# Softmax denominators of a graph-attention and expert kernel: in the last block of queries VectorE adds the weights of the second key head and of every fourth chunk of the first

## The reference

```python
h = _rmsnorm(x, ln1_w)
q = (h @ wq.T)...; k = (h @ wk.T)...; v = (h @ wv.T)...   # 4 query heads, 2 key heads, 32 channels each
scores = jnp.einsum('bhtd,bhsd->bhts', q, k) / jnp.sqrt(jnp.float32(HD))
scores = jnp.where(causal[None, None], scores, jnp.float32(-1e+30))
att = jax.nn.softmax(scores, axis=-1)
y = jnp.einsum('bhts,bhsd->bhtd', att, v)
x = x + y @ wo.T
# then a router picks 2 of 8 experts for each token, and the experts' outputs are added
```

## Time and profile before

| | us |
|---|---|
| median of 3 runs | 4142.93 |
| lowest, highest | 4135.64, 4162.34 |
| the profiled execution, its own time | 4167.11 |
| its span, first to last instruction | 4165.5 |
| TensorE busy (share of the span) | 3452.7 (83%) |
| VectorE busy | 2752.5 (66%) |
| ScalarE busy | 1306.4 (31%) |
| POOL busy | 1638.8 (39%) |
| mean granted TensorE clock, of full | 0.911 |

### The profile page before, as it was taken

How to read it: one execution, slowest core, us unless ns; L and a number is a source line. 1 busy time by engine, 2 the same in 40 slices (tenths; PEclk the granted TensorE clock), 3 DMA queues, 4 the chain that set the end, 5 groups by cost and what they waited for, 6 DMA issues and landing times. The chain is left out here.

```text
span 4165.5 us, 48116 instructions
## 1 busy us (share of the span) xinstructions
PE 3452.7 (83%) x16381; PEld 1324.3 (32%) x16381; DVE 2752.5 (66%) x3882; ACT 1306.4 (31%) x1635; POOL 1638.8 (39%) x1016
## 2 busy tenths in 40 slices
PE   1456899999999859987999899999899999839960
PEld 1233444444444312222222222222222222105540
DVE  8778887614344457777778878777777775326752
ACT  0000000000000014433444455454445455625640
POOL 1000000000000014544766486565478566844551
PEclk8567899999999969999999999999999999969985
DMA  9888998787888436500100000000000000012225
GB/s 372 347 346 346 345 344 319 288 292 284 296 296 291 169 123 236 181 10 5 33 13 6 12 21 8 10 1 10 1 23 9 6 1 6 12 54 65 75 65 181
DMA packets 165282, 572.71 MB, mean 137 GB/s; under 512 B 20193, under 2 KB 55786, under 8 KB 114550
## 3 DMA queue, kind: packets, MB, share of 16 engines
q1 hardware_dynamic: 91304, 457.35, 29.7%
q10 hardware_dynamic: 60432, 88.88, 6.0%
q0 software_dynamic: 13360, 24.03, 1.8%
HBM read 478.22 MB, written 90.57 MB: 137 GB/s over the span
## 5 line engine op out<-in xcount | busy, mean ns | idle before, releaser
L958 DVE TENSOR_REDUCE unit_max<-ps_max 128x1 f32<-128x512 f32 (+3 forms) x2176 | 1356.6, 662 | 424.2 <-PE ps_max L1215 306.6
L786 POOL TENSOR_TENSOR chunk_sum<-chunk_sum,probs 128x1024 f32<-128x1024 f32 (+1 forms) x528 | 1196.1, 2265 | 577.4 <-ACT probs L918 563.2
L918 ACT ACTIVATE probs<-ps_scores 128x1024 f32<-128x1024 f32 (+1 forms) x1088 | 1020.9, 984 | 1057.2 <-PE ps_scores L1234 858.4
L1215 PE MATMUL ps_max<-keep_k_stack,q_stack 96*128 96x512 f16 (+3 forms) x2176 | 762.1, 383 | 154.4 <-DVE unit_max L958 114.1
L1234 PE MATMUL ps_scores<-q_stack,keep_k_stack 97*128 97x512 f16 (+3 forms) x2176 | 616.1, 378 | 36.4 <-ACT probs L918 32.6
L1245 PE MATMUL ps_out<-probs,keep_v 128*32 128x512 f32 (+3 forms) x4352 | 567.2, 594 | 0.6 <-ACT probs L918 0.6
L314 DVE TENSOR_TENSOR partial_degree<-partial_degree,ring 128x2048 f32<-128x2048 f32 x240 | 550.0, 2292 | 7.1
L1215 PEld LDWEIGHTS ps_max<-keep_k_stack,q_stack 96*128 96x128 f16 x2176 | 182.2, 97 | 974.8 <-DVE unit_max L958 822.2
L497 PE MATMUL ps_gather<-ring,keep_attended 128*128 128x512 f32 x960 | 449.2, 630 | 22.1 <-DVE keep_attended L338 22.1
L512 PE MATMUL ps_gather_low<-ring,keep_attended 128*128 128x512 f32 x800 | 362.2, 609 | 1.4 <-DVE keep_attended L338 1.4
L277 POOL DMA_DIRECT2D scratch_lower<-lower x15 | 9.3, 618 | 815.7 <-ACT lower L416 815.7
(11 more groups left out here) (232 smaller groups left out, 2709.7 us busy)
## 6 DMA issues: line engine op xcount, KB each, us to landing
ring<-in_adj SPq DMA_DIRECT2D x392, 1024.0 KB, 6.7
scratch_slots<-empty_rows ACTq DMA_DIRECT2D x16, 2080.0 KB, 7.4
scratch_parts<-empty_part ACTq DMA_DIRECT2D x8, 2048.0 KB, 7.6
moe_parts<-scratch_parts SPq DMA_DIRECT2D x64, 256.0 KB, 3.5
moe_x_rows<-scratch_slots SPq DMA_DIRECT2D x39, 260.0 KB
x_in<-in_x SPq DMA_DIRECT2D x16, 256.0 KB, 6.0
x_in<-in_x ACTq DMA_DIRECT2D x16, 256.0 KB, 9.9
cos<-in_cos ACTq DMA_DIRECT2D x16, 256.0 KB, 8.0
```

The lines of the kernel that those rows point to most:

```text
L786: nc.gpsimd.tensor_tensor(chunk_sum[:, :, lo:], chunk_sum[:, :, lo:], weights, ALU.add).then_inc(chunk_added, 1)
L918: nc.scalar.activation(probs[:, j, kv, :, lo:], ps_scores[kv][:, :, lo:], ACT.Exp, scale=SCALE).then_inc(exp_done, 1)
L958: nc.vector.tensor_reduce(unit_max[:, i, at:at + 1], bank[:, 0:width], AX_X, ALU.max).then_inc(bank_free, 1)
L1215: last = nc.tensor.matmul(out[:, 0:width], q_stack[0:SHIFT_ROW, T % QBUF, h, s * P:(s + 1) * P], k_stack[0:SHIFT_ROW, h // NREP, G * BT:G ...
```

## The change

In the units 121 to 135 (`late_units`, all of the last block but the diagonal) three things differ.

- TensorE no longer calls `add_weights`; `weigh` itself counts `chunk_used` up by one for each chunk.
- VectorE gets `add_late`, after the last of the four steps of each chunk: it adds the chunk's `kv` = 1 weights into the new SBUF tile `late_sums[:, 1]`, and at the fourth chunk also the `kv` = 0 weights into `late_sums[:, 0]`. The first add of each half is a copy. That is 75 operations on 128 x 1024 float32 (73 adds and 2 copies), five for each of 15 units; each add waits for the one before it by `late_added`.
- POOL skips its add at the fourth chunk of each late unit (it only counts the semaphore), so it makes 45 adds there where it made 60.

ScalarE waits for `late_added` before it overwrites a part of `probs` that VectorE reads. At the end of the block TensorE waits for all 75 and adds `late_sums` to the total with four more matmuls.

```diff
--- before.py
+++ after.py
@@ -612,6 +612,8 @@
         paces.append(1 if LAST - 1 in Rs else 2)
         scattered_at.append(routed_at[-1] + 4 * paces[-1])
 
+    late_units = range(first_unit(LAST) + 1, first_unit(NB))
+
     def preparing(unit):
 
         for R in range(LAST):
@@ -649,6 +651,7 @@
         q_stack = sb("q_stack", [STACK, QBUF, NH, BT], F16)
         probs = sb("probs", [P, SUB, NKV, NREP, BT])
         chunk_sum = sb("chunk_sum", [P, NREP, BT])
+        late_sums = sb("late_sums", [P, NKV, NREP, BT])
         zeros = sb("zeros", [SHIFT_ROW, P], F16)
         even_and_odd = sb("even_and_odd", [P, P])
         unit_max = sb("unit_max", [P, TILES, NB + 1])
@@ -702,6 +705,7 @@
         exp_done = sem("exp_done")
         chunk_used = sem("chunk_used")
         chunk_added = sem("chunk_added")
+        late_added = sem("late_added")
         numerator_copied = sem("numerator_copied")
         sums_copied = sem("sums_copied")
         combined = sem("combined")
@@ -841,7 +845,11 @@
             for T in range(NB):
                 for n, G in enumerate(units_of(T)):
                     for j in range(SUB):
-                        add_chunk(T, first_unit(T) + n, j, n == 0)
+                        if first_unit(T) + n in late_units and j == SUB - 1:
+                            pool.wait_ge(chunk_added, (first_unit(T) + n) * SUB + j)
+                            pool.sem_inc(chunk_added, 1)
+                        else:
+                            add_chunk(T, first_unit(T) + n, j, n == 0)
                         route(first_unit(T) + n, j)
             divide(LAST)
             keep_residual(LAST)
@@ -915,6 +923,8 @@
                         act.wait_ge(chunk_used, unit * SUB + (j - SUB + 1))
                         if kv == 0:
                             act.wait_ge(chunk_added, unit * SUB + (j - SUB + 1))
+                        if unit - 1 in late_units and (kv or j == SUB - 1):
+                            act.wait_ge(late_added, (SUB + 1) * (unit - 1 - late_units[0]) + j + 1 + (kv == 0))
                     nc.scalar.activation(probs[:, j, kv, :, lo:], ps_scores[kv][:, :, lo:], ACT.Exp,
                                          scale=SCALE).then_inc(exp_done, 1)
 
@@ -973,6 +983,20 @@
                 if T >= KEPT:
                     dve.wait_ge(block_divided, T - KEPT + 1)
                 nc.vector.tensor_copy(denominators[:, T % KEPT], ps_sum[:]).then_inc(sums_kept, 1)
+
+            def add_late(unit, j):
+
+                first = unit == late_units[0]
+                for kv in ((1, 0) if j == SUB - 1 else (1,)):
+                    dve.wait_ge(exp_done, unit * EXPS + PER_CHUNK * j + kv + 1)
+                    before = (SUB + 1) * (unit - late_units[0]) + j + (kv == 0)
+                    out, weights = late_sums[:, kv], probs[:, j, kv]
+                    if first and (j == 0 or kv == 0):
+                        add = nc.vector.tensor_copy(out, weights)
+                    else:
+                        dve.wait_ge(late_added, before)
+                        add = nc.vector.tensor_tensor(out, out, weights, ALU.add)
+                    add.then_inc(late_added, 1)
 
             def invert(R, s):
                 here = denominators[:, R % KEPT, s * P:(s + 1) * P]
@@ -1171,6 +1195,8 @@
                         if T and v == 0 and i == COMBINE_GAP:
                             keep_denominators(T - 1)
                         route(first_unit(T) + v, i)
+                        if first_unit(T) + v in late_units and i % SUB == SUB - 1:
+                            add_late(first_unit(T) + v, i // SUB)
                 if T == 0:
                     round_shift(1)
             b = len(batches) - 1
@@ -1272,6 +1298,13 @@
                 for r in range(NREP):
                     last = nc.tensor.matmul(ps_sum[r * HD:(r + 1) * HD, :], keep["ones_heads"][:], chunk_sum[:, r, :],
                                             start=False, stop=True, skip_group_check=True)
+                if T == LAST:
+                    pe.wait_ge(late_added, (SUB + 1) * len(late_units))
+                    for kv in range(NKV):
+                        for r in range(NREP):
+                            at = kv * NREP + r
+                            last = nc.tensor.matmul(ps_sum[at * HD:(at + 1) * HD, :], keep["ones_heads"][:],
+                                                    late_sums[:, kv, r, :], start=False, stop=True, skip_group_check=True)
                 last.then_inc(combined, 1)
 
             def project(R):
@@ -1339,7 +1372,8 @@
                     for kv in range(NKV):
                         scores(T, unit, G, 0, kv, True)
                 for j in range(SUB):
-                    paired = not diagonal and j % 2
+                    late = unit in late_units
+                    paired = not diagonal and j % 2 and not late
                     for kv in range(NKV):
                         if j + 1 < SUB:
                             scores(T, unit, G, j + 1, kv, diagonal)
@@ -1350,13 +1384,15 @@
                     pe.wait_ge(exp_done, unit * EXPS + PER_CHUNK * (j + 1))
                     if diagonal and j == 0 and T:
                         pe.wait_ge(numerator_copied, T)
-                    weigh(G, j, diagonal)
+                    last = weigh(G, j, diagonal)
+                    if late:
+                        last.then_inc(chunk_used, 1)
                     if paired:
                         gap(T, v, 4 * j + 1)
                     gap(T, v, 4 * j + 2)
                     if diagonal and j == 2:
                         clear_sums(T)
-                    if j in ((2, 3) if diagonal else (1, 3)):
+                    if j in ((2, 3) if diagonal else (1, 3)) and not late:
                         add_weights(j if j % 2 else j - 1, diagonal).then_inc(chunk_used, 2)
                     if diagonal and j == 0 and T:
                         combine(T - 1, lambda: gap(T, v, 3))
```

## The result

| | before | after |
|---|---|---|
| median of 8 runs, us | 4152.02 | 4185.09 |
| lowest, highest | 4135.64, 4162.34 | 4172.78, 4198.76 |
| the profiled execution, its own time | 4167.11 | 4172.78 |

A forecast was written before the change was run, and what follows sets the result against it. POOL and TensorE were taken as full, POOL alone setting the pace with scatters, and VectorE adds as blocking POOL's. Terms 17.6 - 6.3 + 5.3 gave +16.6, say +17, on the 4143 median: 4160 us, range 4128 to 4188.

The forecast's parts named there:

- units 128 to 133: Last block's units with scatters: 13.4 us each, 80.4 against 86.7, a gain of 6.3 us, VectorE not slowing scatters.
- units 134 and 135: Last block's two late units after the scatters: 25.2 us against 19.86, a loss of 5.3 us.
- units 121 to 127: Last block's late units before the scatters: 100.4 us against 82.8, a loss of 17.6 us.
- Two engines that look free for each other are not: Last block: VectorE operations and POOL adds do not overlap; a 512-element multiplication costs POOL 0.30 to 0.38 us.
- The pair at 3.36 us: Late units: one POOL add and one VectorE add together take 3.36 us, bounds 2.9 to 3.6.
- The lone add at 1.26: Late units: a VectorE add without a POOL add beside it takes 1.22 us plus a 0.04 us hand-over.
- TensorE's relief is worth nothing here: Late units without scatters: dropping add_weights lets ScalarE need 8.1 us instead of 10.06, but 12.6 us of adds bounds them.
- the overlap rival: Last block: long VectorE and POOL adds overlap after all, making the kernel 28 us faster, 4115; chance 0.10.
- The doubled scatter: Scatter units: two scatters now stand behind each other, 2.57 us start to start at best in place of 1.18.
- The signs: Profile marks named beforehand: VectorE adds 2.2 to 3.0 us, POOL's 2.9 to 3.6, ScalarE waiting for late_sums, scatter units shorter.
- The draw: Last block: a pair of adds costs only 2.9 us, about +2 us in all, 4145; chance 0.12.
- the clock rival: Last block: TensorE, less busy, is granted 1.2 GHz and sets the pace, 40 us on top, 4200; chance 0.16.

The follow-up runs named there:

- e2: Changed kernel with the last block's 24 row scatters issued after the first three chunks of units 128 to 135, none after the fourth; ratio to before 1.0052.
- e6: Changed kernel with all eight adds of a late unit on VectorE, none on POOL or TensorE; ratio to before 0.9996.
- e5: Changed kernel with VectorE making head 0's four adds in a late unit, POOL none, TensorE keeping add_weights for head 1; ratio to before 0.9946.

## Why the prediction was right or wrong

The forecast was +17 us at 4160 and a range of 4128 to 4188; measured are +33 and 4185.09. Direction and range held; the size was half, and the range held by 3 us, on a median of before that is now 9 us above the 4143 that the forecast was added to. What failed is the step for units 128 to 133, which was to gain and lost: that put the block 20.5 us off. Misses of 5.2 us in units 134 and 135 and of 2.2 in units 121 to 127 went the other way, so that luck brought the total nearer than its parts. Point by point:

- **Two engines that look free for each other are not.** Right, and shown by e1: the same kernel with reductions, which read one SBUF input, in place of VectorE's adds has a block 36.8 us shorter.
- **The pair at 3.36 us.** 3.29 measured. The lone add at 1.26: 1.33 measured. Full blocking by the lengths before would have been 3.60; the rows of before had the smaller figure. (The Trainium skill, "SBUF — State Buffer", section "Who interferes with whom", has the full blocking; the trace agrees on the blocking and not on its full length.)
- **Units 121 to 127.** Forecast +17.6, measured +15.4. Right: VectorE was busy 93.28 of the 98 us, as the queue-bound sum had it. The parts of that sum (88.2 of adds, 10 of old work, 2.2 of POOL's) were not measured one by one.
- **TensorE's relief is worth nothing here.** Right. e1 adds that in units 121 to 127 it was worth nothing even without the exclusion (82.8 us, as before), so the overlap rival's 28 us would not have come there either. VectorE's queue, which then holds up the old work, is the likely reason; it was not isolated.
- **Units 128 to 133.** This is the step that failed: 13.4 us a unit forecast, 16.8 measured; -6.3 forecast, +14.2 measured. The term was "that VectorE does not slow a scatter down". It rested on the earlier trace rows, where the scatter began at 3803.66 and VectorE's operation at 3803.70, 0.04 us after it. The row shows that an operation that comes later does not disturb a scatter under way; I read it as saying that the two do not meet. In the changed kernel a VectorE operation is first for 19 of the 24: a scatter's issue then takes up to 1.87 instead of 0.98, and the mean of the 24 is 1.58. Against e1's clean 13.79 us, a unit of 17.9 has 0.9 more in its three adds, 2.5 in three scatters, and 0.7 in the doubled pair, together 4.1.
- **The doubled scatter.** I put 2.57 us from start to start, from the earlier trace rows; e1 has 3.1 to 3.2 without VectorE in the way, the changed kernel 3.9. So 0.6 us a unit were missing in any case. e2 confirms the doubled scatter as a cost.
- **Units 134 and 135.** Forecast 25.2, measured 20.0. VectorE is ahead of POOL when the scatters end, so that POOL's six adds, 6 x 3.29, set the time, and VectorE has no lone ones left. The stretch is not a steady state. At 10.0 us a unit it also meets one of the signs that I had named as proving me wrong, a unit without scatters under 11 us. The sign was badly chosen: the pairs themselves took the 3.29 us forecast, and VectorE's lone adds had been made before.
- **The signs.** ScalarE's longest waits were for `late_sums` (28.5 us), as forecast. VectorE's adds had a mean of 2.06 us where 2.2 to 3.0 was named, and the scatter units, named as the one place that gets shorter, lost 14.2 us.
- **The draw, the overlap and the clock.** The draw and the overlap did not come. TensorE's granted clock fell from 0.98 and 0.96 to 0.83 and 0.82, so the observation behind the clock rival was right, but e1 had nearly the same clock (0.86 and 0.83) with the loss gone.

## What to carry to other kernels

An idle VectorE is no free helper for a POOL that reads SBUF. Look in the trace for VectorE operations that end with a POOL instruction, and count the work of both that shows this as one queue: here VectorE's adds with two SBUF inputs, and its copies, with POOL's adds and the starts of its scatters. In these runs it paid to move all of POOL's adds and not a part of them; one or two left on POOL was not tried, and with eight adds on VectorE (e6) the gain was gone. Four adds a unit on VectorE gave +1.0% with POOL at four, and -0.7% with POOL at none and its count off the path. When an engine is relieved of its work but keeps a count in its queue, look at what stands before that count.

## What the runs showed of the hardware that I had not expected

- An indirect DMA issued by POOL waits at its start for a VectorE add with two SBUF inputs that is already under way (1.78 us against 0.98; the scatter ends some 0.86 us after the add), while one that has begun is not held up by a later operation (0.97 us at 3624.07, and the earlier trace rows). With `tensor_reduce`, one SBUF input, the issue stays at 0.98 (e1). What the start of a scatter shares with the add, the runs do not show. The Trainium skill ("SBUF — State Buffer", section "Who interferes with whom") reports a probe in which `tensor_tensor` did not stall DMAs that POOL issues, and infers a reason for it. Here, with indirect DMAs, it does, by 0.8 us, when it comes first.
- Of the exclusion, some 0.3 us per pair of adds is hidden: 2.38 + 1.23 us of work take 3.29 from start to start.
- A chain of scatters that wait for each other runs at 3.1 us a link where no add of VectorE is in the way (e5), and mostly near 4.0 where one is (e6).
